# Row sums by a product with a column of ones, reciprocals spread by a store and a load, result weighted a step later

## The reference, cut to what matters

```python
def _gat_layer(x, W, adj):
    proj = x @ W
    Wh, Ws = jnp.split(proj, 2, axis=-1)
    scores = Wh @ Ws.T
    a = jax.nn.softmax(scores, axis=-1) * adj      # 3327 x 3327
    out = a @ Wh
    out = out + x
    return jax.nn.leaky_relu(out, NEG_SLOPE)
# x: 3327 x 256; called twice, with W_stack[0] and W_stack[1]
```

## Time and profile before

| | |
|---|---|
| Time, median of 3 runs | 1598.15 us (1597.79 to 1599.51) |
| The profiled execution | 1598.0 us, of which the span is 1596.2 us |
| PE busy | 1552.2 us, 97% of the span |
| DVE, ACT, POOL busy | 1140.6, 1075.4 and 968.3 us |
| Granted TensorE clock | 0.998 of full speed |
| DMA | 163.36 MB, 102 GB/s on average |

### The profile page before, as it was taken

The page is one execution under the profiler, slowest core; times in us unless marked ns, Lnnn a source line. Parts: engine busy times, 40 slices in busy tenths (PEclk is TensorE's granted clock), DMA queues, the critical chain, the costliest instruction groups (busy, mean ns, idle before and its releaser), DMA issues.

```text
span 1596.2 us, 34864 instructions
## 1 busy us (share of the span) xinstructions
PE 1552.2 (97%) x12946; PEld 1538.8 (96%) x12946; DVE 1140.6 (71%) x2145; ACT 1075.4 (67%) x2127; POOL 968.3 (61%) x864
## 2 busy tenths in 40 slices
PE   6999999999999999999999999999999999999996
PEld 5999999999999999999999999999999999999996
DVE  7766666766675677777777777756777777777773
ACT  4679989898985566666666666646666666666665
POOL 2112222222220488888888888847888888888884
PEclk9999999999999999999999999999999999999999
DMA  4124444544430133333333334522333333333333
GB/s 149 48 67 120 120 117 116 142 124 119 116 103 27 44 97 100 100 100 100 100 99 98 99 99 151 191 67 76 104 101 100 100 100 100 101 101 104 101 100 93
DMA packets 88666, 163.36 MB, mean 102 GB/s; under 512 B 9265, under 2 KB 19376, under 8 KB 88240
## 3 DMA queue, kind: packets, MB, share of 16 engines
q1 hardware_dynamic: 60624, 113.41, 24.2%
q0 software_dynamic: 24336, 44.31, 11.3%
q10 hardware_dynamic: 3536, 3.41, 0.7%
HBM read 147.99 MB, written 13.11 MB: 101 GB/s over the span
## 4 chain that ended last, share of the span: by engine, by line
PE 83%; issue 6%; DVE 5%; POOL 3%; ACT 2%; DMA 0%; SPq 0%; POOLq 0%; DVEq 0%; ACTq 0%
PE PS L1236 29%; PE PS L1448 8%; PE PS L1451 8%; PE PS L1450 8%; PE PS L1311 5%; PE PS L1308 5%; PE PS L1310 5%; PE PS L1309 5%; PE PS L1307 5%; POOL FR L467 2%; POOL X L460 1%; DVE AF L1052 1%; DVE AF L982 1%; ACT FR L650 1%; DVE PS L1092 1%
## 5 line engine op out<-in xcount | busy, mean ns | idle before, releaser
L467 POOL TENSOR_TENSOR FR<-AF,FR 128x512 fp32r<-128x512 f32 x338 | 451.7, 1336 | 139.0 <-ACT FR L650 134.1
L1236 PE MATMUL PS<-FR,RB 128*128 128x256 f32 x3900 | 515.9, 281 | 1.8 <-ACT X L616 1.8
L1236 PEld LDWEIGHTS PS<-FR,RB 128*128 128x128 f32 x3900 | 481.6, 188 | 3.1 <-ACT X L616 3.0
L460 POOL TENSOR_TENSOR X<-X,ROW 128x512 f32<-128x512 f32 x283 | 369.7, 1307 | 81.9 <-ACT ROW L660 81.9
L1448 PE MATMUL PS<-FR,RA 128*128 128x256 f32 x1300 | 372.7, 287 | 7.3 <-POOL FR L467 5.9
L1451 PE MATMUL PS<-FR,RA 128*128 128x256 f32 x1300 | 365.0, 281 | 0.0
L1450 PE MATMUL PS<-FR,RA 128*128 128x256 f32 x1300 | 364.3, 280 | 0.0
L1052 DVE TENSOR_TENSOR AF<-PS,AJ 128x512 f32<-128x512 f32 x338 | 231.4, 685 | 80.3 <-ACT PS L628 69.6
L425 POOL DMA_DIRECT2D STGT<-adjt x169 | 90.2, 534 | 292.9 <-PE PS L1311 292.9
L616 ACT ACTIVATE X<-PS 128x512 f32<-128x512 f32 x272 | 161.9, 595 | 142.2 <-DVE AF L982 136.8
L1448 PEld LDWEIGHTS PS<-FR,RA 128*128 128x128 f32 x1300 | 244.6, 188 | 13.3 <-POOL FR L467 11.7
(11 more groups left out here) (174 smaller groups left out, 2455.2 us busy)
## 6 DMA issues: line engine op xcount, KB each, us to landing
AJ<-adjt SPq DMA_DIRECT2D x338, 256.0 KB, 2.7
STGT<-adjt POOLq DMA_DIRECT2D x169, 256.0 KB, 3.0
xt_scratch<-ROW SPq DMA_DIRECT2D x12, 512.0 KB, 2.7
RB<-xt_scratch SPq DMA_DIRECT2D x12, 512.0 KB, 4.7
x_scratch<-X ACTq DMA_DIRECT2D x13, 256.0 KB, 2.1
ROW<-x_scratch SPq DMA_DIRECT2D x13, 256.0 KB, 3.1
out<-ROW SPq DMA_DIRECT2D x12, 256.0 KB, 3.3
X<-xt SPq DMA_DIRECT2D x1, 1536.0 KB, 11.5
```

Of the source, the lines that this page charges most:

```text
L460: nc.gpsimd.tensor_tensor(slot, slot, MB.unsqueeze(1).broadcast_to([P, 2, 256]), ALU.subtract)\
L467: nc.gpsimd.tensor_tensor(LO[g % 2], WA[g % 2], HI[g % 3].bitcast(F32), ALU.subtract)\
L1236: last = nc.tensor.matmul(out, stationary(a, k), moving(b, k), start=(k == 0 and i == 0), stop=(k == K - 1 and i == 2))
```

## The change

For 23 of the 25 blocks that pass this way ("far" blocks; `NEAR` holds the last block of the first layer, b = 12, and b = 24), the row sums' reciprocals no longer pass over TensorE and ScalarE but are stored to DRAM by SP as 128x2 numbers and loaded back as 256 numbers on every partition. `weighted` and all that follows it come one step later for them (`R_END` in place of `A_END`). For all 25 blocks the transposition with the sum behind it is replaced by a product: `turn_sum` multiplies the 128x128 sums (as the stationary operand) by a column of ones, so that two columns of PSUM hold the row sums, and `row_sum` takes the reciprocal from there.

```diff
+NEAR = (PAIRS - 1, LB - 1)
+def nears(b):
+    return sum(i <= b for i in NEAR)
+def fars(b):
+    return b + 1 - nears(b)
+FAR_END = {v: b for v, b in A_END.items() if b not in NEAR}
+R_END = {v + (b not in NEAR): b for v, b in A_END.items()}
...
+        rec_dram = nc.dram_tensor("rec_scratch", [LAYERS * PAIRS, 2 * P], F32).ap()
...
+            def store_rec(b):
+                sp.wait_ge(rec_d, b + 1)
+                sp.dma_start(rec_dram[b, :].rearrange("(p h) -> p h", h=2), RC).then_inc(rec_st, 16)
+
+            def load_rec(b):
+                sp.wait_ge(rec_st, 16 * fars(b))
+                if b:
+                    sp.wait_ge(y_d, b)
+                sp.dma_start(RINB, rec_dram[b, :].partition_broadcast(P)).then_inc(rec_in, 16)
...
+                if v - 1 in FAR_END:
+                    load_rec(FAR_END[v - 1])
+                if v in FAR_END:
+                    store_rec(FAR_END[v])
...
-                    if v == max(CH - UNITS + u + 1, UNITS * u + UNITS - 1 + LAG + 4):
+                    if v == max(CH - UNITS + u + 1, UNITS * u + UNITS - 1 + LAG + 5):
                         load_x2(u)
...
-                if A_END.get(v) is not None:
+                if A_END.get(v) in NEAR:
                     spread_rec(A_END[v])
...
             def row_sum(b):
                 dve.wait_ge(t3_mm, b + 1)
-                nc.vector.reduce_sum(DC, PS[:, 7, 0:256].rearrange("p (h j) -> p h j", h=2), AX)\
-                  .then_inc(dsum_d, 1)
-                dve.wait_ge(dsum_d, b + 1)
-                if b:
-                    dve.wait_ge(bcr_d, b)
-                nc.vector.reciprocal(RC, DC).then_inc(rec_d, 1)
+                if fars(b - 1):
+                    dve.wait_ge(rec_st, 16 * fars(b - 1))
+                if nears(b - 1):
+                    dve.wait_ge(bcr_d, nears(b - 1))
+                nc.vector.reciprocal(RC, PS[:, 7, 0:2]).then_inc(rec_d, 1)
...
-                if A_END.get(v - 1) is not None and v - 1 != LAST1:
-                    weighted(A_END[v - 1])
+                if R_END.get(v - 1) is not None and v - 1 != LAST1:
+                    weighted(R_END[v - 1])
...
                 for h in range(2):
-                    last = nc.tensor.transpose(PS[:, 7, h * P:(h + 1) * P], DN2[:, h * P:(h + 1) * P], IDN[:, :])
+                    last = nc.tensor.matmul(PS[:, 7, h:h + 1], DN2[:, h * P:(h + 1) * P], ONE, start=True, stop=True)
                 last.then_inc(t3_mm, 1)
...
-                if A_END.get(v) is not None and v != LAST1:
+                if A_END.get(v) == LB - 1:
                     turn_sum_back(A_END[v])
```

More of the change, by code:

```diff
@@ L170, in two_graph_blocks @@
         PADB = COL[:, 22:23]
+        ONE = COL[:, 23:24]
         NMX = COL[:, 34:36]
@@ L270, in two_graph_blocks @@
         t3_mm = sem("t3_mm")
-        dsum_d = sem("dsum_d")
         rec_d = sem("rec_d")
+        one_set = sem("one_set")
+        rec_st = sem("rec_st")
+        rec_in = sem("rec_in")
         bcr_d = sem("bcr_d")
@@ L396, in _ @@
                     load_x1(b)
-                b = A_ALL.get(v - 4)
+                b = R_END.get(v - 4)
                 if b is not None and b >= PAIRS:
                     store_out(b)
+                if v == a_step(NG - 1) + 4:
+                    store_out(LB)
             sp.wait_ge(out_stored, 32)
@@ L411, in _ @@
             nc.gpsimd.memset(NHALF, -0.5).then_inc(half_set, 1)
+            nc.gpsimd.memset(ONE, 1.0).then_inc(one_set, 1)
             pool.wait_ge(pad0, 1)
@@ L666, in keep_rec @@
             def keep_rec(b):
-                act.wait_ge(t4_mm, b + 1)
-                if b:
-                    act.wait_ge(y_d, b)
+                act.wait_ge(t4_mm, nears(b))
+                act.wait_ge(y_d, b)
                 nc.scalar.activation(RINB, PS[:, 7, 256:512], ACT.Copy).then_inc(rinb_d, 1)
@@ L740, in _ @@
                     keep_max(S_END[v - 2])
-                if A_END.get(v - 1) is not None and v - 1 != LAST1:
-                    keep_rec(A_END[v - 1])
+                if A_END.get(v - 1) == LB - 1:
+                    keep_rec(LB - 1)
                 if x is not None and x < GL:
@@ L764, in _ @@
                     nc.scalar.activation(WX[:, 0, :, 0:D], WRAW1[:, 1, :, 0:D], ACT.Copy).then_inc(w_hi, 1)
-                b = A_END.get(v - 2)
+                b = R_END.get(v - 2)
                 if b is not None and b < PAIRS - 1:
@@ L1014, in last_sum @@
                 dve.wait_ge(lexp_d, UNITS)
-                dve.wait_ge(bcr_d, LB)
+                dve.wait_ge(bcr_d, len(NEAR))
                 nc.vector.reduce_sum(DC, ESUM[:, :, :], AX).then_inc(lsum_d, 1)
@@ L1071, in row_sum @@
                 dve.wait_ge(t3_mm, b + 1)
-                nc.vector.reduce_sum(DC, PS[:, 7, 0:256].rearrange("p (h j) -> p h j", h=2), AX)\
-                  .then_inc(dsum_d, 1)
-                dve.wait_ge(dsum_d, b + 1)
-                if b:
-                    dve.wait_ge(bcr_d, b)
-                nc.vector.reciprocal(RC, DC).then_inc(rec_d, 1)
+                if fars(b - 1):
[3 more added lines that the diff above has]
+                nc.vector.reciprocal(RC, PS[:, 7, 0:2]).then_inc(rec_d, 1)
             def weighted(b):
                 dve.wait_ge(av_mm, UNITS * (b + 1))
-                dve.wait_ge(rinb_d, b + 1)
-                y = acc1(b)
-                nc.vector.tensor_tensor(y, y, RINB.unsqueeze(1).broadcast_to([P, K, 256]), ALU.mult).then_inc(y_d, 1)
+                if b in NEAR:
+                    dve.wait_ge(rinb_d, nears(b))
+                else:
+                    dve.wait_ge(rec_in, 16 * fars(b))
+                rec = RINB.rearrange("p (h j) -> p h j", h=2) if b in NEAR else RINB.rearrange("p (j h) -> p h j", h=2)
+                y = acc1(b).rearrange("p k (h j) -> p k h j", h=2)
+                nc.vector.tensor_tensor(y, y, rec.unsqueeze(1).broadcast_to([P, K, 2, P]), ALU.mult).then_inc(y_d, 1)
             def residual(b, s):
@@ L1171, in _ @@
                     maximum(e)
-                if A_END.get(v - 1) is not None and v - 1 != LAST1:
-                    weighted(A_END[v - 1])
+                if R_END.get(v - 1) is not None and v - 1 != LAST1:
+                    weighted(R_END[v - 1])
                 if x is not None:
                     mask(x)
-                if A_END.get(v - 1) is not None and v - 1 != LAST1:
-                    residual(A_END[v - 1], 0)
+                if R_END.get(v - 1) is not None and v - 1 != LAST1:
+                    residual(R_END[v - 1], 0)
                 if e == NG - 1:
@@ L1189, in _ @@
                     last_result()
-                if A_END.get(v - 1) is not None and v - 1 != LAST1:
-                    residual(A_END[v - 1], 1)
+                if R_END.get(v - 1) is not None and v - 1 != LAST1:
+                    residual(R_END[v - 1], 1)
                 if S_END.get(v - 1) is not None:
@@ L1223, in _ @@
                     xt_low(PAIRS - 1)
-                b = A_END.get(v - 3)
+                b = R_END.get(v - 3)
                 if b is not None and b >= PAIRS:
@@ L1511, in turn_sum @@
                     pe.wait_ge(xt_lo, UNITS)
-                elif b <= PAIRS:
-                    pe.wait_ge(rinb_d, b)
-                else:
+                    pe.wait_ge(one_set, 1)
+                else:
+                    pe.wait_ge(rec_d, b)
+                if b == PAIRS:
+                    pe.wait_ge(rinb_d, 1)
+                if b > PAIRS:
                     pe.wait_ge(res_d, b - PAIRS)
                 for h in range(2):
-                    last = nc.tensor.transpose(PS[:, 7, h * P:(h + 1) * P], DN2[:, h * P:(h + 1) * P], IDN[:, :])
+                    last = nc.tensor.matmul(PS[:, 7, h:h + 1], DN2[:, h * P:(h + 1) * P], ONE, start=True, stop=True)
                 last.then_inc(t3_mm, 1)
             def turn_sum_back(b):
-                pe.wait_ge(bcr_d, b + 1)
+                pe.wait_ge(bcr_d, nears(b))
                 for h in range(2):
@@ L1527, in turn_out @@
                 pe.wait_ge(y3_d, b + 1)
-                pe.wait_ge(rinb_d, b + 1)
+                pe.wait_ge(rec_d, b + 1)
+                if b == LB - 1:
+                    pe.wait_ge(rinb_d, len(NEAR))
                 for h in range(2):
```

2 lines of the change are left out of this document (1 added, 1 removed).

## The result

The changed kernel takes 1704.9 us (median of 4 runs, 1702.0 to 1706.7), the kernel before 1598.7: a ratio of 1.066, 95% interval 1.065 to 1.068. It is slower by 106 us, and the forecast of 1600.4 us (1591 to 1613) was wrong.

A forecast was written before the change was run, and what follows sets the result against it. It took TensorE to bound the second layer, and a late chain per block starting when reciprocals arrive the first. First layer 0.1, crowded block 1.0, second layer 1.1: +2.2 us on 1598.0, median 0.15 above, 1600.4 us (1591 to 1613).

The forecast's parts named there:

- the one on the store: Landing time of the 1 KB reciprocals' store to DRAM: taken as 1.75 us, ends 1.5 and 3.3.
- The round trip is long: Rival, chance 0.30, slower: 8-byte pieces may land in 2.3 us, load 2.8, R = 5.1, giving 1612 us.
- The load: Bringing the reciprocals back from DRAM, 128 KB behind an adjacency load: taken as 2.75 us, ends 2.1 and 3.1.
- R: Time from the reciprocal's end to the start of `weighted`: 1.51 us before, forecast 4.6, ends 3.7 and 6.5.
- the product of E+3: Second layer, TensorE's product after the delayed mask's low part: start T0 + 4.22 + R, wanted at T0 + 8.78.
- T0: In each block, the start of the first transpose of the sums (700.38 in block 3); the forecast's times count from it.
- the late product: First layer, TensorE's product waiting for POOL's low part: forecast at T0 + 10.98 + R; that step's product before started at T0 + 15.57.
- the prediction's own rules: A first-layer block changes by R - 4.59 us; a second-layer block lengthens by R - 4.5 where R exceeds 4.5.
- TensorE's own program: TensorE's work: 5.3 us saved by dropping transposes back, 5.8 added by products with ones; even at +0.5 us.
- the rival of the short round trip: Rival, chance 0.27, faster: store lands in 1.5 us, load in 2.4, R = 4.0, giving 1591 us.
- the crowded block: First layer's end (b = 10), where both DMAs queue among 512 KB loads of the next layer's x: 1 us added once.
- The cap: First layer: TensorE's floor limits the gain to about 1 us a block, which would give 1586 us.

The follow-up runs named there:

- the filled kernel: The changed kernel with 36 idle identity transposes where TensorE stands still in every far block: 1690.7 us against 1704.9.
- the 512-byte store: The changed kernel storing 128 x 512 bytes of unreduced sums instead of 128 x 8 bytes (result not the reference's): 1623.4 us, ratio 1.016.

## Why the prediction was wrong

**The step that failed** is the one on the store: "That is the lower end; the upper is 3.3, [...] I take 1.75." It lands in 4.8 us. The value came from a line through 256 and 512 KB in pieces of 2 KB and more, drawn down to 1 KB; the rival "The round trip is long" saw the 8-byte pieces and gave them 2.3. The load is the second error of the same step: 2.75 taken, 3.5 measured, most likely because the adjacency load ahead of it is held up too and lands 4.9 us after its issue (block 3). With 512-byte pieces the two take 2.1 and 3.0, near enough to 1.75 and 2.75. The upper end of R, 6.5, lay in the working and was left out of the range; even it would have been too low for a mean R of 8.35. The figure of the Trainium skill (DMA: Bandwidth & Descriptors, Anatomy of one DMA) that the prediction set beside its own, 2.0 us and little more for 1 KB, is given there for transfers issued by GpSimd. The small stores of the other arrangements, issued by SP, agree with it here with 2.0 us; the 128 neighbours of 8 bytes with their 4.8 do not.

**What was right: the chain behind `weighted`.** "the product of E+3 can start at T0 + 0.85 + R + 0.60 + 2.77 = T0 + 4.22 + R" holds in both layers. With the measured R of 9.15 us in block 3 and 8.40 in block 16 it gives T0 + 13.4 and T0 + 12.6; the trace has T0 + 13.2 and T0 + 12.5, and no other product of these blocks waits for 0.1 us or more. For the first layer the prediction had put the stall at another product ("the late product comes at T0 + 0.85 + R + 10.13 = T0 + 10.98 + R"). That one starts at T0 + 20.3 in block 3, where the form gives 20.1, but TensorE is not idle before it. So in the first layer the place of the stall was wrong and its size right, because the two forms differ by under 0.1 us.

With each block's measured R in the prediction's own rules, and the reciprocals ready at T0 + 0.71 as measured in place of 0.85, the sum is 12 x (R - 4.59) + 11 x (R - 4.5) - 23 x 0.14 = 84 us. For the filled kernel (mean R of 8.50) the same rules give 88, and its span grew by 91. With the 512-byte store (mean R of 5.62) they give 21.5, for 24.4. So the rules are right to 3 us, and the forecast failed by what was put in for R: 4.6 us, with 1.3 us of waiting for `weighted` where 4.9 were measured.

**What was missing: the clock.** No term of the sum had it, since TensorE's stalls were to stay under 1 us, and with stalls of that length the kernel before runs at a clock of 0.998. The span of the changed kernel grew by 104 us, 20 more than the 84 of the rules; 3 of these the filled kernel has as well, and the other 17 went with the half clock. Most of them fall in the second layer, where TensorE's program is everything: it grew by 55.5 us in its blocks b = 13 to 23 and by 44.7 with the fill, the first layer by 48.7 and 46.3.

**TensorE's own program** was right: the pair of products holds the next one for 0.36 us where the transposes hold it for 0.14, 0.22 more for a forecast of 0.23 more (0.45 against 0.22); the transposes back were priced at 5.3 us and brought 5.8; together it is even. The pair leaves four records of weight loads, two a call, as in L1351. A load for each of the four passes that the Trainium skill (FP8 and Floating Point Precision, TensorE Precision Notes) states, the upper bound of 0.9 us, did not show. Two small slips of the working change nothing: the 0.14 us of a single weight load are in the trace (473.11, L1363) but not in the earlier trace rows, and the rival of the short round trip leaves out the 1 us of the crowded block that the forecast adds.

**The late step's worth** was not seen. The sum took R as the only unknown and stopped at step E+2. By its own terms the wait ends at T0 + 0.85 + R, and the second layer was said to be TensorE's program alone, so a place some steps later was free. That was the gain that the kernel had to offer, 7 us at one step later and 12 at three, both with the old way. The cap that the prediction had named, about 1 us a block in the first layer, is what was there to win: with the weighting three steps later its twelve blocks take 12.1 us less.

## What to carry to other kernels

A DMA round trip costs nothing or everything, depending on whether the instruction that waits for it stands before or after its landing in its engine's order: a store of 4.8 us with a load of 3.5 to 3.8 behind it made 1704.9 us at one place and 1587.4 at a place two steps later. Read from the trace what is queued behind the waiting instruction, and move the wait until the longest plausible landing is covered. And price a transfer from one with pieces of the same size in the same arrangement; here a line through large transfers gave 1.5 us for 128 pieces of 8 bytes side by side that took 4.8.

## What the runs showed of the hardware

- A store of 128 x 8 bytes to DRAM, side by side, lands in 4.8 us (medians of 4.4 to 5.0 in the six kernels that have it). The same pieces at a distance of 512 bytes, pieces of 64, 256 and 512 bytes side by side, and 8-byte pieces to the SBUF all land in 2.0 to 2.1. The difference lies behind the last packet.
- While the slow store is on its way, a 256 KB load issued from the same or another queue lands in about 5 us (medians of 5.1 over 23 loads) in place of 2.7.
- After a stall of TensorE of 3 to 4 us the granted clock was 0.50 for a stretch of about 3.4 us (in the window 724.6 to 728.0 all of it), and filling the stall with idle transposes gained 14 us.
- VectorE's reciprocal of 128x256 from PSUM takes 1.76 us, of 128x2 0.17.
- An fp32 product with one column is two weight loads a call, and a pair of them delays the next product by 0.36 us, a pair of transposes by 0.14.
